# The probabilities of the cross attention: normalised on POOL, in one product with the broadcast reciprocal

## The chip, the cores and the metric

The kernel runs on one core of a Trainium2 chip. The metric is the time of one execution on the device, in microseconds (us). The core has five engines that matter here: TensorE (PE; its weight loads are listed as PEld), VectorE (DVE), ScalarE (ACT), GpSimd (POOL), and SyncE (SP), which issues most of the DMAs. Each engine works through its own queue in order, and the queues are tied by semaphores.

## What is computed

One decoder layer on x of 8 x 112 x 512 with a context of 8 x 375 x 512, all float32:

```python
x = x + attn(layernorm(x))                 # 16 heads of 32, rotary, causal
x = x + xattn(layernorm(x), ctx)           # below
x = x + ffn(layernorm(x))                  # ternary weights, silu gate

# xattn: 16 heads of 128 in 8 groups; self part and cross part, then one projection
q, k, v = fp8-quantised projections of ln(x);   q, k layer-normed
core = softmax(q k^T / sqrt(128)) v                      # over 112 tokens
kx, vx = projections of ctx;  qx, kx layer-normed
xout = softmax(qx kx^T / sqrt(128)) vx                   # over 375 context rows
out  = quantise(concat(core, xout)) @ wproj^T * scales
```

The change is in the softmax of the cross part: 8 batches x 16 heads = 128 matrices of 112 x 375.

## The kernel before, in words

The program has three stretches. Until about 210 us it does the first attention. Then come the self parts and the cross parts of the second attention, each in two halves of the heads ("halves" S0, S1, X0, X1; X0 from about 470 to 785 us, X1 to about 1095 us), each half over 8 batches. The feed-forward part follows, and its first steps overlap the end of X1.

In the stretch with the halves a planner in Python emits everything. It walks through ticks. In each tick it goes through the list `order` (L1333) and emits, for each entry (kind, lag, function), the step of the item that is due by that lag. Since each engine has one queue and works in order, the order of emission is the order of work. Per tick there is one item of projection (`p_...`), one head of attention (`t_...`) and sometimes a background unit (`b_...`) that prepares weights. In a cross half a batch has 8 projection items (q0, q1, k0, k1, k2, v0, v1, v2) and 8 heads, so it takes 8 ticks.

The steps of one cross head, with their lags behind the tick of the head:

- `t_s0` (lag 0): PE makes the scores (L1000), DVE their negated maximum (L1002), ACT the exponential with its sum (L1003) into a buffer `p` of the ring `pr`, which has two slots.
- `t_s1` (lag 1): DVE takes the reciprocal of the sum (L1017) and scales `p` with it (L1023) into a buffer `hl` of the ring `hlr`, two slots. Then the slot of `pr` and that of the small numbers (`small2`, 5 slots) are released.
- `t_s2` (lag 3): PE transposes `hl` in three pieces (L1035); DVE copies them (L1052) in X0, ACT (L1050) in X1.
- `t_s3` (lag 4): product with v (L1070), once for two heads. `t_s4` (lag 5): every fourth head, quantisation of the result (`quant`, L665: DVE L672 to L675, POOL L676 and one or two of L678). `t_s6` (lag 8): projection (L1122), once a batch.

The steps of the projection: PE L891 or L901, DVE statistics (L415, L418), `p_rstd` with ACT L426, L427 and POOL L432, L433 (for q and k, not for v), then ACT L830 and, transposed (L841), L847.

The background units of kind "t" prepare ternary weights of the feed-forward part: PE L356, ACT L359, DVE L369 to L371, POOL L372 and L373, all of `b_2` from L369 on, then DVE L380. In X0 and the first batch of X1 four ticks of eight have such a unit. The units of kind "w" split weights into two bf16 parts; for some of them POOL does the subtraction (L340, in `b_1`).

What POOL gets in one tick is thus, in the order of `order`: L432 and L433 (`p_rstd`), L676 and L678 (`t_s4`), L372 and L373 (`b_2`), anything from `t_s1`, and L340 (`b_1`). PE gets L1035, L1000, L841, L1122, L1070, L891 or L901, and L356.

PSUM has eight banks of 512 columns, taken from one pool in the order in which they come free; a bank of the scores is released by the exponential L1003.

Of the kernel before, what the change touches and what calls it, by code (L numbers as in the profile page):

```python
# [9 lines left out]
ALU = mybir.AluOpType  # L10
# [4 lines left out]
T = 112  # L15
# [105 lines left out]
def decoder_layer(nc, x, ctx_t, w_a, w_s, w_x, w_p, w_g, w_d, vec, bias, cst, cst2, scr, xs, out):  # L121
    ctx = ExitStack()
    with ctx:
        def sem(name):
            return ctx.enter_context(nc.semaphore(name))
# [4 lines left out]
        pe, act, dve, pool = (Queue(sem(f"s_{n}")) for n in ("pe", "act", "dve", "pool"))  # L130
# [842 lines left out]
        def p_head(p, hh):  # L973
            v = p[0:T, 120 * hh:120 * hh + 119]
            return bass.AP(v.tensor, v.offset, [list(v.ap[0]), [17, 7], [1, 16]])
# [35 lines left out]
        def t_s1(it):  # L1011
            S = it["bt"]["k"] == "S"
            sm, p = it["sm"], it["p"]
            n = 2 if S else 1
            w = T if S else SC
            ri = sm[0:T, 4:4 + n]
            tr = dve(lambda e: e.reciprocal(ri, sm[0:T, 2:2 + n]), it["te"])  # L1017
            hi_i, hl, hf = hlr.take()
            for j in range(n):
                dst, src = hl[0:T, w * j:w * j + w], p[0:T, w * j:w * j + w]  # L1020
                if S:
                    dst, src = dst.rearrange("p (a n) -> p a n", a=7), p_head(p, j)
                tl = dve(lambda e, j=j, dst=dst, src=src: e.tensor_scalar(  # L1023
                    dst, src, ri[:, j:j + 1], None, ALU.mult), tr, hf)
            pr.release(it["pi"], tl)
            small2.release(it["mi"], tl)
            it.update(hl=hl, hli=hi_i, tl=tl)
# [302 lines left out]
        for u in bg[LEAD + 7][16:]:  # L1330
            u["free"] = lambda: a_end
        spill_ring = Ring([f32(a, 256) for a in (aFR, aFR + 256, aCX, aCX + 256)])
        order = [("p", 1, p_stats), ("p", 1, p_vhi), ("a", 3, t_s2), ("a", 0, t_s0), ("p", 1, p_rstd), ("a", 5, t_s4),  # L1333
                 ("p", 3, p_t), ("b", 6, b_4), ("b", 3, b_2), ("a", 1, t_s1), ("p", 1, p_z), ("a", 8, t_s6),
                 ("a", 4, t_s3), ("p", 0, p_mm), ("b", 2, b_m), ("b", 4, b_3), ("b", 1, b_1), ("b", 0, b_0)]
        every = tuple(range(8))
# [167 lines left out]
```

How the kernel before makes its waits and increments, by code:

```python
    def emit(self, eng):  # L63
        for need, make, inc in self.items:
            last = {}
            for t in need:
                last[id(t.sem)] = t
            for t in last.values():
                eng.wait_ge(t.sem, t.value)
            ins = make(eng)
            if inc:
                ins.then_inc(self.sem, 1)
# [1331 lines left out]
        def run_dma(eng, items):  # L1404
            for waits, dst, src, s in items:
                for t in waits:
                    eng.wait_ge(t.sem, t.value)
                eng.dma_start(dst, src).then_inc(s, 16)
# [1 line left out]
        @block.sync  # L1410
        def _(eng):
            run_dma(eng, sync_items)
            eng.wait_ge(s_out, 16 * (NB - 1))
```

## Time and profile before

| | |
|---|---|
| time, median of 3 runs | 1215.86 us (1215.51 to 1218.77) |
| the profiled execution, its own time | 1215.43 us |
| its span, first to last instruction | 1213.1 us |
| PE busy | 1150.4 us (95%) |
| DVE busy | 920.6 us (76%) |
| ACT busy | 809.5 us (67%) |
| POOL busy | 608.9 us (50%) |
| mean granted TensorE clock | 0.983 of full speed |

The durations below come from the profiled execution, whose time differs from the median by 0.4 us. Its own time is 2.3 us more than its span. A busy PE is one with a matmul in flight. The granted clock is told as a share of 2.4 GHz.

### The profile page before, as it was taken

What the parts mean: (1) busy time and instruction counts of PE and PEld (TensorE: products, weight loads), DVE (VectorE), ACT (ScalarE), POOL (GpSimd) and SP (SyncE); (2) the same over time, 40 slices, a digit from 0 to 9 for tenths busy, and PEclk for the clock granted to TensorE, in tenths of its full rate; (3) what the DMA queues carried; (4) which work ended last, traced back from release to release, by engine and by line L of the source; (5) the groups of instructions that cost most, each with busy time, mean ns of one, the idle gap of its engine ahead of it and who ended that gap; (6) DMA issues with size and microseconds to landing.
All of it is one profiled execution on the core that took longest, in us unless ns stands there. A gap on an engine that the chain in (4) does not pass through costs nothing.

```text
span 1213.1 us, 19327 instructions
## 1 busy us (share of the span) xinstructions
PE 1150.4 (95%) x6330; PEld 764.5 (63%) x6330; DVE 920.6 (76%) x2801; ACT 809.5 (67%) x2316; POOL 608.9 (50%) x769
## 2 busy tenths in 40 slices
PE   4889988789999999999999999999999999999998
PEld 2657756556666666666666766667666666554564
DVE  4668977999878876898999989987887546586252
ACT  4667658777878876677667766678776678566140
POOL 1546984653544555454566656444544112257172
PEclk9989989899999999999999999999999999999999
DMA  8220010211211221213232232226111000000000
GB/s 273 88 60 25 26 34 17 86 51 56 70 36 36 60 84 48 79 43 108 92 113 77 69 103 74 78 70 208 61 44 52 1 2 1 1 1 1 36 1 27
DMA packets 30788, 72.41 MB, mean 60 GB/s; under 512 B 3184, under 2 KB 12528, under 8 KB 30688
## 3 DMA queue, kind: packets, MB, share of 16 engines
q1 hardware_dynamic: 30416, 70.82, 18.5%
q8 instruction: 50, 0.82, 0.3%
q14 instruction: 50, 0.41, 0.1%
q10 hardware_dynamic: 272, 0.36, 0.1%
HBM read 62.78 MB, written 8.39 MB: 59 GB/s over the span
## 4 chain that ended last, share of the span: by engine, by line
PE 59%; DVE 19%; ACT 12%; POOL 7%; issue 1%; DMA 1%; ACTq 0%; POOLq 0%; SPq 0%
PE ps L901 14%; PE ps L1194 8%; PE ps L1122 8%; PE ps L891 7%; PE ps L1070 5%; PE ps L1000 4%; PE ps L1263 4%; ACT big L830 4%; PE ps L1035 3%; PE ps L841 3%; DVE big L415 2%; DVE big L1023 2%; POOL big L699 2%; DVE big L243 1%; POOL big L698 1%
## 5 line engine op out<-in xcount | busy, mean ns | idle before, releaser
L901 PE MATMUL ps<-big 128*125 128x512 bf16 x1152 | 264.6, 379 | 1.4 <-ACT big L830 1.3
L830 ACT ACTIVATE big<-ps,big 112x128 f32<-112x128 f32 (+1 forms) x512 | 192.8, 456 | 71.6 <-POOL big L433 68.9
L901 PEld LDWEIGHTS ps<-big 128*125 128x125 bf16 x1152 | 155.1, 136 | 81.9 <-ACT big L830 1.9
L432 POOL TENSOR_TENSOR big<-big 112x4 f32<-112x4 f32 (+1 forms) x128 | 37.5, 293 | 327.2 <-ACT big L427 327.1
L891 PE MATMUL ps<-big 128*112 128x512 bf16 x768 | 187.9, 388 | 5.4 <-ACT big L994 2.1
L891 PEld LDWEIGHTS ps<-big 128*112 128x112 bf16 x768 | 100.1, 133 | 70.7 <-issue 7.7
L1003 ACT ACTIVATE big<-ps,big 112x375 f32<-112x375 f32 x128 | 74.6, 583 | 91.0 <-DVE big L1002 90.3
L415 DVE BATCH_NORM_STATS2 big<-ps 112x6 f32<-112x128 f32 (+1 forms) x512 | 113.2, 283 | 20.3 <-PE ps L901 17.3
L1070 PE MATMUL ps<-big 125*128 125x224 f32 (+1 forms) x512 | 121.1, 359 | 5.3 <-DVE big L1052 4.3
L1023 DVE TENSOR_SCALAR big<-big 112x112 f32<-112x112 f32 (+1 forms) x256 | 120.0, 490 | 6.8
L1000 PE MATMUL ps<-big 128*112 128x375 f32 x256 | 102.1, 480 | 0.9 <-ACT big L830 0.9
L1070 PEld LDWEIGHTS ps<-big 125*128 125x128 f32 (+1 forms) x512 | 91.4, 191 | 17.2 <-DVE big L1052 6.1
L1122 PE MATMUL ps<-big 128*128 128x512 bf16 x448 | 101.2, 379 | 1.0 <-ACT big L994 0.9
L1194 PE MATMUL ps<-big 128*128 128x512 bf16 (+1 forms) x512 | 99.1, 352 | 0.0
L676 POOL TENSOR_TENSOR big<-big 128x448 f32<-128x448 bf16 x64 | 62.9, 982 | 70.1 <-DVE big L1017 67.3
L1035 PEld LDWEIGHTS ps<-big 112*125 112x125 f32 (+1 forms) x512 | 78.5, 175 | 30.2 <-DVE big L1023 4.2
L847 ACT ACTIVATE big<-ps,big 128x448 f32<-128x448 f32 (+1 forms) x128 | 94.4, 737 | 0.0
L1002 DVE TENSOR_REDUCE big<-ps 112x1 f32<-112x375 f32 x128 | 68.2, 533 | 34.4 <-PE ps L1000 34.1
L1035 PE MATMUL ps<-big 112*125 112x112 f32 (+1 forms) x512 | 85.2, 268 | 1.7 <-DVE big L1023 1.6
L678 POOL TENSOR_TENSOR big<-big 128x448 bf16<-128x448 f32 (+6 forms) x112 | 82.7, 756 | 5.0
L510 PE MATMUL ps<-big 128*112 128x512 bf16 x288 | 74.9, 409 | 7.5 <-DVE big L243 4.2
L1194 PEld LDWEIGHTS ps<-big 128*128 128x128 bf16 x512 | 50.0, 98 | 45.9 <-issue 0.9
(122 smaller groups left out, 2323.6 us busy)
## 6 DMA issues: line engine op xcount, KB each, us to landing
big<-in_ctx_t SPq DMA_DIRECT2D x32, 375.0 KB, 3.4
big<-in_w_s SPq DMA_DIRECT2D x16, 512.0 KB, 4.4
big<-in_w_p SPq DMA_DIRECT2D x16, 512.0 KB, 4.3
big<-in_w_x SPq DMA_DIRECT2D x16, 512.0 KB, 3.7
big<-in_w_g SPq DMA_DIRECT2D x16, 512.0 KB, 4.0
scr<-big SPq DMA_DIRECT2D x36, 128.0 KB, 1.7
big<-scr SPq DMA_DIRECT2D x9, 512.0 KB, 8.6
big<-in_w_d SPq DMA_DIRECT2D x8, 512.0 KB, 4.8
```

The source lines that it names most:

```text
L415: t = dve(lambda e, j=j: e.bn_stats(st[:, j, :], src[0:rows, width * j:width * j + width]), toks, free)
L678: t5 = pool(lambda e, dst=dst, lo=lo, hi=hi: e.tensor_tensor(dst, t3[:, :, lo:hi], m3[:, :, lo:hi], ALU.subtract), t4, free_dst)
L830: t = act(lambda e, j=j: e.activation(z[0:rows, 128 * j:128 * j + 128], bk[0:rows, 128 * j:128 * j + 128], ACT.Identity, bias=rr[0:rows, 4 ...
L847: tf = act(lambda e: e.activation(dst, b3, ACT.Identity, bias=bb, scale=w), t, free_dst, t_qsb)
L891: t = pe(lambda e, k=k, s=s, n=n: e.matmul(bk[0:T, :], xq[:, k, :], w[:, s, k, col:col + 512], start=n == 0, stop=n == 7), xq_tok[(v, b)], ...
L901: t = pe(lambda e, k=k, s=s, u=u, n=n: e.matmul(bk[0:CK, :], cT[:, s, k, CK * c:CK * c + CK], w[:, u, k, col:col + 512], start=n == 0, sto ...
L1000: t = pe(lambda e: e.matmul(bk[0:T, 0:SC], q[:, h, :], kk[:, g, :], start=True, stop=True), bt["ready"], free)
L1023: tl = dve(lambda e, j=j, dst=dst, src=src: e.tensor_scalar(dst, src, ri[:, j:j + 1], None, ALU.mult), tr, hf)
L1035: t = pe(lambda e, j=j: e.transpose(bb[0:rows, T * j:T * j + T], hl[0:T, rows * j:rows * j + rows], identf[0:T, 0:T]), it["tl"], free, sig ...
L1070: t = pe(lambda e, c=c: e.matmul(bk[:, o:o + 224], v[0:rows, c, 128 * g:128 * g + 128], pT[0:rows, 224 * c:224 * c + 224], start=c == 0, s ...
L1122: t = pe(lambda e, h=h, s=s, n=n: e.matmul(bk, cat[:, h, :], hf["wp"][:, s, h, :], start=n == 0, stop=n == 15), tile["toks"], free, ready[ ...
L1194: t = pe(lambda e, k=k, s=s, n=n, bk=bk, which=which: e.matmul(bk[:, 0:w], wg[:, k, 2048 * which + 128 * m:2048 * which + 128 * m + 128], ...
```

## The change

In `t_s1` the scaling of the cross heads leaves DVE. Instead of DVE's tensor_scalar, with the reciprocal as the scalar of each partition, POOL does one tensor_tensor product of `p` with the reciprocal broadcast over 375 columns. The reciprocal itself stays on DVE. The new product waits for the reciprocal, for the exponential (`it["te"]`) and for its slot of `hlr`; the slots of `pr` and `small2` are now released by POOL. The self heads (S) keep their two scalings on DVE. Nothing else is touched: 128 instructions of DVE become 128 of POOL, at the place that `t_s1` has in the order.

```diff
@@ -1016,12 +1016,14 @@
             ri = sm[0:T, 4:4 + n]
             tr = dve(lambda e: e.reciprocal(ri, sm[0:T, 2:2 + n]), it["te"])
             hi_i, hl, hf = hlr.take()
-            for j in range(n):
-                dst, src = hl[0:T, w * j:w * j + w], p[0:T, w * j:w * j + w]
-                if S:
-                    dst, src = dst.rearrange("p (a n) -> p a n", a=7), p_head(p, j)
-                tl = dve(lambda e, j=j, dst=dst, src=src: e.tensor_scalar(
-                    dst, src, ri[:, j:j + 1], None, ALU.mult), tr, hf)
+            if S:
+                for j in range(2):
+                    tl = dve(lambda e, j=j: e.tensor_scalar(
+                        hl[0:T, w * j:w * j + w].rearrange("p (a n) -> p a n", a=7), p_head(p, j), ri[:, j:j + 1],
+                        None, ALU.mult), tr, hf)
+            else:
+                tl = pool(lambda e: e.tensor_tensor(hl[0:T, 0:w], p[0:T, 0:w], ri.broadcast_to([T, w]), ALU.mult),
+                          tr, it["te"], hf)
             pr.release(it["pi"], tl)
             small2.release(it["mi"], tl)
             it.update(hl=hl, hli=hi_i, tl=tl)
```

## Rows read from the trace of the kernel before

**Rows 1.** The page: busy us, share of the span and instructions of each engine.

```profile
PE 1150.4 (95%) x6330; PEld 764.5 (63%) x6330; DVE 920.6 (76%) x2801; ACT 809.5 (67%) x2316; POOL 608.9 (50%) x769
```

**Rows 2.** Stretches: length; busy of PE, PEld, DVE, ACT, POOL; granted clock; DMA share, GB/s.

```profile
628.00:667.00 39.00, 38.65 (x200) 26.38 (x198) 36.11 (x107) 26.97 (x69) 22.27 (x26) 1.00 0.29 88
892.00:929.00 37.00, 37.00 (x191) 25.50 (x190) 28.65 (x93) 26.87 (x71) 17.69 (x24) 1.00 0.14 42
965.00:1002.00 37.00, 37.00 (x192) 25.68 (x191) 20.85 (x80) 25.64 (x70) 6.69 (x16) 1.00 0.00 1
```

**Rows 3.** Waits: waiting line, releaser: us in total, times, longest us.

```profile
POOL big L432 <- ACT big L427: 327.1, 121, 17.8
...
PE ps L1070 <- DVE big L1052: 4.3, 4, 1.5
...
PE ps L1035 <- DVE big L1023: 1.6, 4, 0.5
```

**Rows 4.** Groups by form, DVE: busy us, mean ns of one | idle before.

```profile
L1023 DVE TENSOR_SCALAR big<-big 112x375 f32<-112x375 f32 x128 | 83.8, 655 | 4.6
```

**Rows 5.** Groups by form, POOL.

```profile
L540 POOL TENSOR_TENSOR big<-big 112x256 f32<-112x256 f32 x32 | 27.9, 893 | 0.0
...
L1239 POOL TENSOR_TENSOR big<-big 128x384 f32<-128x384 f32 x15 | 12.4, 827 | 8.7 <-DVE big L1230 8.7
```

**Rows 6.** Instructions in time, DVE: start, us taken, what [idle before <-releaser].

```profile
602.99 0.42 DVE L1023 TENSOR_SCALAR big<-big 112x375 f32<-112x375 f32 x1
...
619.76 1.33 DVE L1023 TENSOR_SCALAR big<-big 112x375 f32<-112x375 f32 x1
```

**Rows 7.** Instructions in time, POOL.

```profile
497.47 1.16 POOL L373 TENSOR_TENSOR big<-big 128x512 bf16<-128x512 bf16 x1
...
604.88 1.15 POOL L373 TENSOR_TENSOR big<-big 128x512 bf16<-128x512 bf16 x1
...
607.63 0.87 POOL L433 TENSOR_SCALAR big<-big 125x4 f32<-125x4 f32 x1
...
612.26 0.68 POOL L432 TENSOR_TENSOR big<-big 125x4 f32<-125x4 f32 x1 [1.40 <-ACT big L427]
...
616.28 1.53 POOL L372 TENSOR_TENSOR big<-big 128x512 bf16<-128x512 bf16 x1
617.89 1.48 POOL L373 TENSOR_TENSOR big<-big 128x512 bf16<-128x512 bf16 x1
619.73 1.15 POOL L372 TENSOR_TENSOR big<-big 128x512 bf16<-128x512 bf16 x1 [0.36 <-DVE big L1017]
...
859.46 1.19 POOL L678 TENSOR_TENSOR big<-big 128x64 bf16<-128x64 f32 x2
```

**Rows 8.** Instructions in time, PE.

```profile
84.52 0.77 PE L631 MATMUL ps<-big 112*112 112x32 f32 x3 [3.77 <-DVE big L619]
...
497.50 0.48 PE L1035 MATMUL ps<-big 112*125 112x112 f32 x3
...
547.45 2.28 PE L1070 MATMUL ps<-big 125*128 125x224 f32 x6 [1.10 <-DVE big L1052]
...
616.75 0.48 PE L1035 MATMUL ps<-big 112*125 112x112 f32 x3
...
628.83 0.80 PE L1000 MATMUL ps<-big 128*112 128x375 f32 x2
...
859.03 0.48 PE L1035 MATMUL ps<-big 112*125 112x112 f32 x3
```

**Rows 9.** Instructions in time, ACT.

```profile
606.16 0.59 ACT L1003 ACTIVATE big<-ps,big 112x375 f32<-112x375 f32 x1
...
631.41 0.57 ACT L1003 ACTIVATE big<-ps,big 112x375 f32<-112x375 f32 x1 [1.84 <-DVE big L1002]
```

**Rows 10.** Stretches, columns as in rows 2.

```profile
547.00:552.00 5.00, 4.55 (x14) 3.16 (x15) 3.51 (x10) 4.11 (x9) 2.30 (x2) 0.66 0.88 266
84.50:90.00 5.50, 5.48 (x20) 4.01 (x21) 4.82 (x8) 2.98 (x12) 4.68 (x4) 0.50 0.06 25
```

## The prediction

> **What bounds the kernel now.** I read the page first, then the stages, the waits, and last the order of instructions of one batch on each engine. The page says that TensorE (PE) is busy 95% of 1213.1 us at a granted clock of nearly full speed [rows 1]. The stages show where the change falls. While a batch of the first cross half runs, PE is busy 38.65 of 39 us, VectorE (DVE) 36.11 and POOL 22.27; in the second half PE is at 37.00 of 37, and DVE falls from 28.65 to 20.85 once the background work has ended, with POOL at 6.69 [rows 2]. So PE ends every batch; DVE stands close behind it in the first half and far behind in the second. The waits agree: PE waited 1.6 us in all for L1023, the line that is changed, and 4.3 for the copy L1052 [rows 3]. Two things follow. Time taken from DVE can be worth only what PE waits for DVE, and anything that makes PE wait is lost in full.
>
> **Part 1, what leaves DVE.** 128 scalings of 112x375 leave it: mean 655 ns, 83.8 us of busy time in all [rows 4]. They lie beside PE's work. Their price on the path is the 1.6 us in which PE waited for them [rows 3]; I credit 1.6. The self parts keep their two scalings per item and their order, and the reciprocal L1017 stays on DVE, so they cost nothing new; what hides them is unchanged.
>
> **Part 2, the new product on POOL.** No row shows a 112x375 product with a broadcast second operand. From below: the 128x384 product L1239 took a mean of 827 ns, so 375 columns are 0.81 us. From above: the rotary product L540, 112x256 with a broadcast sine, took a mean of 893 ns, which by columns is 1.31 for 375 [rows 5]. Both means hold collisions with DVE. I take 0.90, nearer to L1239, whose operands are plain rows as here; the range keeps 0.81 to 1.31. 128 x 0.90 = 115 us more on POOL. That is 8 x 0.9 = 7.2 us in a batch, so POOL goes from 22.3 to 29.5 of 39 us [rows 2]: by busy time there is room. Busy time isn't what decides, though; the queue is.
>
> **Part 3, where it stands in the queues.** POOL works in the order of emission. In each tick that order is: the two small steps L432 and L433 of the layer norm; the three steps L676, L678, L678 of a quantisation (every fourth head); the ternary subtract and add L372, L373, where a background unit is due; then t_s1's product of the head of the tick before; then L340. On DVE the scaling stood behind the ternary steps of DVE and was done early. On POOL it stands behind L373. Behind the new wait (for L1017 and L1003) only L340 and the next tick's L432 are queued, and the reciprocal is ready long before POOL gets there: the scaling behind it began at 602.99, and POOL's L373 of that tick ended at 604.88 + 1.15 = 606.03 [rows 6, 7]. So the added wait itself costs nothing. What costs is the place. Three parties wait for the product: PE's transposes L1035 two ticks on, the exponential L1003 two heads on (pr has two slots, freed by the product), and the ring hlr.
>
> Take the fourth batch, which stands for the pattern. Its fourth head's transposes start on PE at 616.75 [rows 8], and PE didn't wait for the scaling there. POOL, in the queue ahead of the new product, has seven instructions from 612.26 on, and the last, L373, ends at 617.89 + 1.48 = 619.37 [rows 7]. With 0.08 to the next start (as from 616.28 + 1.53 = 617.81 to 617.89) and 0.90 the product ends at 620.35: PE waits 3.6 us. This isn't cured by a faster product; POOL is 2.6 us late before it even begins. The same subtraction (end of L373, plus 0.98, less the start of L1035) for the nine batches in which a ternary unit meets a quantisation, at the fourth head (the third in the first batch), gives 2.1, 3.1, 3.9, 3.6, 3.7, 3.3, 3.7, 2.6 and 2.6; the first is 497.47 + 1.16 + 0.98 - 497.50 [rows 7, 8]. Sum 28.6. Once PE has waited, the heads that follow are covered: the next one would be late by 2.3 us by the same working, less than the 3.6 already given. After the ninth batch the ternary units are thinner. One place is left, the last of ten: 859.46 + 1.19 + 0.98 - 859.03 = 2.6 [rows 7, 8]. From 965 us on POOL has time to spare (6.69 busy of 37 us [rows 2]) and the product is hidden; if that cover went, 0.9 per head would be the price. Stalls: 31.2 us.
>
> **Part 4, what a stall does to PE's clock.** At 547.45 PE starts after 1.10 us of waiting [rows 8]. In the 5 us from 547 on the granted clock has a mean of 0.66 [rows 10], so for part of them the lower of its two levels, 1.2 in place of 2.4 GHz; 0.34 x 5 = 1.7 us of work lost. After PE's 3.77 us stall before 84.52 [rows 8] the clock was 0.50 for all of the next 5.5 us [rows 10]. So I expect stalls of 3 us to bring the low clock. I charge 1.7 us to nine of the ten stalls, the first of 2.1 us left out: 15.3.
>
> **Sum.** 31.2 + 15.3 - 1.6 = 44.9. The profiled execution took 1215.43 (span 1213.1 and 2.3 around it), the median of the three runs was 1215.86, so the profile stands for them within 0.4. 1215.4 + 44.9 = 1260.3.
>
> **What the sum leaves out**, in both directions. Down: with the scaling gone DVE is earlier. L1003 now starts at 631.41 where its scores began on PE at 628.83, 2.6 us before [rows 8, 9]; the scores need 0.80 of that and the maximum on DVE about 0.6; so up to 1.1 us per batch may come back, 11 in all. Up: the second head of a batch frees pr at 606.03 + 0.98 = 607.0, for an exponential that started at 606.16 [rows 7, 9], 0.9 late, and the third head likewise; that delays L427 and so POOL's L432 behind it, by up to 1.7 per batch, 15 in all. I let the two cancel.
>
> The Trainium skill (SBUF — State Buffer, Who interferes with whom) has a rule on such pairs: a VectorE tensor_scalar in a 2-port mode and any GpSimd instruction exclude each other, and whoever is first holds the pair to its end. The trace agrees: L1023 took 0.42 at 602.99 and 1.33 at 619.76, where POOL's L372 had begun at 619.73 and held it for 1.15 [rows 6, 7]. By that rule the move takes one party of such collisions away, for POOL too: L433 took 0.87 at 607.63, while a scaling ran on DVE [rows 7]. At up to 0.6 for one of them in each of ten batches the sum would be 1254 in place of 1260.
>
> **The rivals.** (a) *Late product, with the low clock*: the forecast, 1260. For it: the order in the queue is fixed by the code, and POOL is late before the product starts. Against it: one execution's spacing. (b) *Late product, clock mostly held*: 1215.4 + 29.6 - about 5 of the give-back = 1240. For it: the trace shows few stalls, and no rule for the fall. Against it: both stalls of rows 8 were followed by it. (c) *POOL becomes the bound of the first half*: exponential, L427, L432 to L373, product, next exponential is a ring from tick to tick. With 1.7 us more per batch, the product at 1.31 and two low stretches for one stall: 44.9 + 15 + 4 + 15 = 79, 1294. Against it: three ticks of each batch have no such chain, and PE lets POOL catch up. (d) *Absorbed*: PE's transposes find their product in time because DVE, relieved, runs the whole ring about 3 us earlier; -1.6 and a stall or two left over, 1216. For it: DVE loses 5 us of work per batch (8 x 0.655). Against it: POOL waits for L427 on ACT, not for DVE [rows 3]. The Trainium skill (Perfetto Trace Analysis, Optimizing Scalar/DVE Operations) warns that moving work between these two engines might not help since they share a port; its outcome, gain and loss alike, would be this one. (e) *Faster*: all that PE waits for DVE's L1023 and L1052 goes, 1.6 + 4.3 = 5.9 us [rows 3], and no transposes are late; 1209.5. It decides only if POOL reaches the product before PE reaches L1035 in the quantisation tick, 3.6 us sooner than now. (f) The change doing nothing is excluded: all 128 heads take the new branch.
>
> **How the numbers follow.** (a) 0.60, (b) 0.20, (c) 0.10, (d) 0.06, (e) 0.04. A measurement of this kernel tells 0.3%, 3.6 us, from no change. (a), (b), (c) are slower: 0.90; (d) same: 0.06; (e) faster: 0.04. Predicted is (a), 1260. The range goes from 1230, just below (b) with all 11 us given back and no low clock (1215.4 + 29.6 - 11 = 1234), to 1285, in the lower part of (c). Outside are (d), (e) and most of (c), under 2 in 10.
>
> **What would show it.** In the trace after: the waits list PE L1035 for POOL with some 30 us in ten or so long waits of 2.5 to 4.5 us, all between 495 and 860 us; the product at 0.81 to 0.95 us when free; the chain of waits through POOL's L372, L373, L676 and L678 once per batch; the granted clock at 0.5 for 3 us after each; batches of the first half 42 to 43 us apart in place of 38, those after 965 us still 36.7. Wrong would be: L1035 never waiting for POOL; waits at PE for banks (L841, L1000 for ACT) in its place, which would mean that the ring of pr bites first; or batches after 965 us longer, which would mean that POOL's place costs even where nothing stands ahead of it.

## The result, and the profile after

The changed kernel took 1247.02 us (median of four runs, 1244.78 to 1248.37) against 1215.94 for the kernel before: ratio 1.0252, 95% interval 1.0237 to 1.0267. That is 31.1 us slower. The profiled execution took 1246.97 us, its span is 1245.0, 31.9 more than before [rows 1]. In the changed kernel the scaling on POOL is L1025; lines behind it have moved by two, so the transposes are L1037, the copy L1054, the product with v L1072. The experiments move them again: in their rows a wait of the transposes for the product always has the form PE ps L10xx <- POOL big L10xx.

The page of the changed kernel, busy time of each engine:

```profile
span 1245.0 us, 19667 instructions
PE 1152.6 (93%) x6330; PEld 760.6 (61%) x6330; DVE 894.2 (72%) x2673; ACT 813.3 (65%) x2316; POOL 688.1 (55%) x897
```

PE was idle 1245.0 - 1152.6 = 92.4 us, before 1213.1 - 1150.4 = 62.7 [rows 1]: 29.7 of the 31.9 us are PE standing still. Who it waited for is in the waits of the changed kernel (waiting line, releaser: us in total, times, longest):

```profile
POOL big L432 <- ACT big L427: 284.2, 121, 8.2
...
ACT big L1003 <- POOL big L1025: 66.1, 55, 3.5
...
PE ps L1037 <- POOL big L1025: 30.2, 23, 2.9
```

L1037 waited 30.2 us for the new product, where L1035 had waited 1.6 for DVE [rows 3]. The exponentials, L1003, waited another 66.1, a row that doesn't exist before. Stretches of the changed kernel that answer to rows 2 (length; busy of PE, PEld, DVE, ACT, POOL; granted clock):

```profile
643.00:682.00 39.00, 35.97 (x183) 24.24 (x182) 32.49 (x91) 26.18 (x65) 26.12 (x34) 1.00 0.23 70
937.00:974.00 37.00, 36.15 (x184) 24.51 (x183) 24.86 (x82) 25.22 (x68) 21.19 (x31) 1.00 0.14 42
997.00:1034.00 37.00, 37.00 (x192) 25.61 (x191) 17.28 (x72) 25.57 (x70) 12.77 (x24) 1.00 0.00 1
```

Most of the loss is in the first cross half (PE 35.97 of 39 us where it was 38.65 [rows 2]): 22.7 us of the 30.2 us of waits. The other 7.5 are in the first part of the second half, and nothing in its last part, where the ternary units have ended: PE 37.00 of 37 with POOL's work nearly doubled. POOL isn't full in any of these stretches: 26.12 of 39 us.

The batch that answers to the one shown before, POOL in order of time (start, us taken):

```profile
621.32 0.20 POOL L432 TENSOR_TENSOR big<-big 125x4 f32<-125x4 f32 x1 [1.26 <-ACT big L427]
621.60 0.37 POOL L433 TENSOR_SCALAR big<-big 125x4 f32<-125x4 f32 x1
621.94 1.16 POOL L676 TENSOR_TENSOR big<-big 128x448 f32<-128x448 bf16 x1
623.18 1.45 POOL L678 TENSOR_TENSOR big<-big 128x128 bf16<-128x128 f32 x2
624.58 1.20 POOL L372 TENSOR_TENSOR big<-big 128x512 bf16<-128x512 bf16 x1
625.86 1.48 POOL L373 TENSOR_TENSOR big<-big 128x512 bf16<-128x512 bf16 x1
627.30 0.99 POOL L1025 TENSOR_TENSOR big<-big 112x375 f32<-112x375 f32 x1
```

and PE and ACT at the same place:

```profile
628.34 0.58 PE L1037 MATMUL ps<-big 112*125 112x112 f32 x3 [2.86 <-POOL big L1025]
```

```profile
620.15 0.57 ACT L1003 ACTIVATE big<-ps,big 112x375 f32<-112x375 f32 x1 [0.60 <-POOL big L1025]
...
628.38 0.57 ACT L1003 ACTIVATE big<-ps,big 112x375 f32<-112x375 f32 x1 [3.22 <-POOL big L1025]
```

Here is the whole ring of one tick, a circle of steps in which each waits for the one before: exponential at 620.15, L427, POOL from 621.32 to 628.29 without a pause, then the next exponential at 628.38, whose slot of `pr` the product has just freed. That is 8.2 us, and PE and ACT both stand at its end.

### The profile page after: what moved, and what is told of

Same layout as the page of the kernel before. It is cut to its first block, busy times and chain, and to the rows that moved or that the text cites. A ratio compares the mean times of both kernels' runs of the same rounds, so it can differ in the third digit from the quotient of the medians.

```text
span 1245.0 us, 19667 instructions
## 1 busy us (share of the span) xinstructions
PE 1152.6 (93%) x6330; PEld 760.6 (61%) x6330; DVE 894.2 (72%) x2673; ACT 813.3 (65%) x2316; POOL 688.1 (55%) x897
## 4 chain that ended last, share of the span: by engine, by line
PE 54%; POOL 16%; DVE 15%; ACT 11%; issue 2%; DMA 1%; ACTq 0%; POOLq 0%; SPq 0%
PE ps L901 11%; PE ps L1196 8%; PE ps L1124 8%; PE ps L891 7%; PE ps L1072 5%; PE ps L1000 4%; PE ps L1265 4%; PE ps L1037 3%; ACT big L830 3%; POOL big L373 2%; POOL big L1025 2%; PE ps L841 2%; ACT big L1003 2%; POOL big L372 2%; DVE big L415 2%
## 5 line engine op out<-in xcount | busy, mean ns | idle before, releaser
L432 POOL TENSOR_TENSOR big<-big 112x4 f32<-112x4 f32 (+1 forms) x128 | 34.6, 271 | 284.3 <-ACT big L427 284.2
L1003 ACT ACTIVATE big<-ps,big 112x375 f32<-112x375 f32 x128 | 73.8, 577 | 143.3 <-DVE big L1002 75.4
L415 DVE BATCH_NORM_STATS2 big<-ps 112x6 f32<-112x128 f32 (+1 forms) x512 | 113.2, 283 | 28.3 <-PE ps L901 22.7
L1025 POOL TENSOR_TENSOR big<-big 112x375 f32<-112x375 f32 x128 | 112.7, 883 | 36.0 <-DVE big L1017 36.0
L1072 PE MATMUL ps<-big 125*128 125x224 f32 (+1 forms) x512 | 120.1, 357 | 4.1 <-DVE big L1054 3.2
L1037 PEld LDWEIGHTS ps<-big 112*125 112x125 f32 (+1 forms) x512 | 76.7, 175 | 66.5 <-POOL big L1025 43.6
L1037 PE MATMUL ps<-big 112*125 112x112 f32 (+1 forms) x512 | 87.3, 272 | 30.5 <-POOL big L1025 30.2
L1072 PEld LDWEIGHTS ps<-big 125*128 125x128 f32 (+1 forms) x512 | 90.9, 190 | 15.3 <-DVE big L1054 4.2
L678 POOL TENSOR_TENSOR big<-big 128x448 bf16<-128x448 f32 (+6 forms) x112 | 78.3, 717 | 5.0
```

The source lines that it names most:

```text
L415: t = dve(lambda e, j=j: e.bn_stats(st[:, j, :], src[0:rows, width * j:width * j + width]), toks, free)
L1003: te = act(lambda e: e.activation(p[0:T, 0:SC], bk[0:T, 0:SC], ACT.Exp, bias=sm[0:T, 0:1], accum_out=sm[0:T, 2:3]), tm, pf)
L1025: tl = pool(lambda e: e.tensor_tensor(hl[0:T, 0:w], p[0:T, 0:w], ri.broadcast_to([T, w]), ALU.mult), tr, it["te"], hf)
L1037: t = pe(lambda e, j=j: e.transpose(bb[0:rows, T * j:T * j + T], hl[0:T, rows * j:rows * j + rows], identf[0:T, 0:T]), it["tl"], free, sig ...
L1072: t = pe(lambda e, c=c: e.matmul(bk[:, o:o + 224], v[0:rows, c, 128 * g:128 * g + 128], pT[0:rows, 224 * c:224 * c + 224], start=c == 0, s ...
```

## The experiments

The theory after this look was *place*: the loss is PE waiting for a product that stands behind other work in POOL's queue. The first rival was *load*: 113 us more work on POOL and its collisions with DVE, wherever the product stands. Later the theory was split: *fixed place* (only what stands ahead of the product in its own tick counts, as the prediction's sum had it) against *ring* (each tick's product also delays the next exponential and with it POOL's next tick). Each round of runs timed the kernel before again on the same chip, with medians of 1214.68, 1214.81 and 1215.61 us; every cost below is the difference to the one of its own round, and "came back" is what is missing from the 31.1 us.

**The product ahead of the ternary steps.** Steps for cross heads alone are called `s1_cross`, the self heads stay where they were.

```diff
-                 ("p", 3, p_t), ("b", 6, b_4), ("b", 3, b_2), ("a", 1, t_s1), ...
+                 ("p", 3, p_t), ("b", 6, b_4), ("a", 1, s1_cross), ("b", 3, b_2), ("a", 1, s1_self), ...
```

> Edit to the changed kernel: for the cross heads the step t_s1 (reciprocal on DVE, product on POOL) is emitted before the ternary steps of the tick (L372, L373 on POOL), still behind L432, L433 and the quantisation. Theory 'place' (the 31 us are PE waiting for a product that stands behind L373): in the tick that held PE longest the product now ends 2.4 us sooner, so of the 2.5 to 2.9 us of each long wait 0 to 0.5 is left; PE waits for POOL's product under 5 us in all, time 1214 to 1222. Rival 'load' (the cost is 113 us more work on POOL and its collisions with DVE, wherever it stands): the product is as long and as frequent, time stays at 1235 to 1247.

Measured: 1243.02 us, ratio 1.0236 (1.0220 to 1.0251). I was wrong: the cost is 28.3 us, some 3 less than before the move, and the two intervals overlap (1.0237 to 1.0267 for the changed kernel), so even that gain isn't clear. The waits, and the quantisation tick of the fifth batch (the one above was of the fourth):

```profile
PE ps L1037 <- POOL big L1025: 16.0, 19, 3.2
```

```profile
663.02 0.33 POOL L432 TENSOR_TENSOR big<-big 125x4 f32<-125x4 f32 x1 [2.17 <-ACT big L427]
663.43 0.22 POOL L433 TENSOR_SCALAR big<-big 125x4 f32<-125x4 f32 x1
663.62 1.47 POOL L676 TENSOR_TENSOR big<-big 128x448 f32<-128x448 bf16 x1
665.17 1.36 POOL L678 TENSOR_TENSOR big<-big 128x192 bf16<-128x192 f32 x2
666.49 1.26 POOL L1025 TENSOR_TENSOR big<-big 112x375 f32<-112x375 f32 x1
```

The product's inputs are old by then (its exponential was one tick before), yet POOL stands idle for 2.17 us at L432, which waits for ACT's newest work, and the product stands behind it and behind the quantisation. L373 was only part of the queue that matters; PE's waits for the product fell from 30.2 to 16.0, and others took part of their place (L1072 for the copy 4.9, L841 for ACT 2.0 us). These rows don't account for all of the time: why 14 us less of this wait gave only some 3 us stays open.

**The product first in its tick.**

```diff
-                 ("a", 3, t_s2), ("a", 0, t_s0), ("p", 1, p_rstd), ... ("a", 1, t_s1), ...
+                 ("a", 3, t_s2), ("a", 1, s1_cross), ("a", 0, t_s0), ("p", 1, p_rstd), ... ("a", 1, s1_self), ...
```

> Edit to the changed kernel: for the cross heads t_s1 is emitted directly behind t_s2, so POOL's product stands first in its tick, ahead of L432, L433, the quantisation and the ternary steps. Theory 'place': PE never waits for the product, exponentials hardly do; time 1210 to 1217, at or a little under the kernel before since DVE is relieved. What could spoil it: L432 now stands behind a product that waits for its slot of hlr (PE's transposes) and so ACT's L830 may come 0.8 us later; then 1216 to 1222 with waits for POOL's L433. Rival 'load': 1235 to 1247.

Measured: 1216.72 us, ratio 1.0013 (1.0002 to 1.0023). From its waits and from POOL's order:

```profile
PE ps L1037 <- POOL big L1025: 0.9, 2, 0.5
```

```profile
609.06 0.81 POOL L1025 TENSOR_TENSOR big<-big 112x375 f32<-112x375 f32 x1 [0.67 <-DVE big L1017]
610.63 0.33 POOL L432 TENSOR_TENSOR big<-big 125x4 f32<-125x4 f32 x1 [0.75 <-ACT big L427]
```

Now the product lies in time in which POOL waited for L427 anyway. The cost is 2.0 us by the medians, 0.13% by the ratio, so 29 of the 31 us are gone, with the same instructions on the same engines. *Load* falls for this kernel as the cause of the 31 us.

**The same order with the scaling on DVE**, the control.

> Edit to the kernel before: the same move of t_s1 for the cross heads as in the run e2_early (directly behind t_s2), with the scaling still on DVE. It shows what the order alone is worth. Theory 'place': the scaling was early enough already, PE waited 1.6 us for it in all, and now DVE's maximum stands behind it by 0.4 to 0.6 us; time 1212 to 1222, so that a difference between e2_early and this run is the engine's, not the order's. Rival ('order': moving t_s1 early is by itself worth 10 us or more): under 1206 here.

Measured: 1231.97 us, ratio 1.0142 (1.0126 to 1.0157): 17 us slower than the kernel before, outside what I expected. Two rows name waits that are new or longer:

```profile
L1023 DVE TENSOR_SCALAR big<-big 112x375 f32<-112x375 f32 x128 | 84.1, 657 | 24.4 <-PE ps L1035 20.3
```

```profile
PE ps L901 <- ACT big L1003: 3.7, 7, 0.9
```

In this place the scaling needs the slot of hlr that PE's transposes of the same tick release, and DVE stood 20.3 us behind that. But all fifteen of these waits lie behind 850 us, none in the first half, where the batches had grown too, from 38 to 39 us. There the new wait is PE's for a PSUM bank that an exponential frees (six of the seven lie there): DVE's maximum now stands behind the scaling, so the exponential comes later. PE never waited for the scaling itself. How the 17 us divide between the two isn't shown, and the last batch alone, beside the first feed-forward steps, took 8 us more. So the early order isn't good by itself: it cost 17 us with the scaling on DVE and 2 with it on POOL. What e2_early gained is not an effect of the order alone.

**Extra load that nobody waits for.** DVE scales as before; POOL does one more product from constants. In a second run (e9_shadow_first) it is emitted behind `t_s0` and ahead of `p_rstd`, so that it is the first of its tick on POOL, and waits for the exponential in place of the reciprocal.

```diff
+            if not S:
+                shadow[0] = pool(lambda e: e.tensor_tensor(f32(aFR + 512, SC)[0:T], big[0:T, aCF:aCF + SC],
+                                 cf[0:T, C_UNIT:C_UNIT + 1].broadcast_to([T, SC]), ALU.mult), tr, shadow[0])
             pr.release(it["pi"], tl)
```

> Edit to the kernel before: DVE still scales; beside that POOL does one more product of 112x375 with a broadcast column for each cross head, from constants into a spare area, at the place in POOL's queue at which the change puts its product. Nobody waits for it. It changes nothing of the result. Theory 'place': POOL is as loaded as in the changed kernel (some 690 us) but PE waits for no product; time 1214 to 1222, the few us being L432 and L340 behind it and DVE's two-input steps blocked by it. Rival 'load': DVE keeps its 84 us and POOL has 113 more, so all collisions are there and more: 1240 or above.

> Edit to the kernel before: the extra POOL product of the run e4_shadow (nobody waits for it, DVE still scales), now emitted first in its tick, ahead of L432. The earlier run had it behind the ternary steps and took 23 us. Theory 'place and DVE': POOL's load is the same, but the product no longer stands in one row with L372 and L373 against DVE's scaling; it can start before L427 is done, in POOL's idle time. Time 1216 to 1226. Rival 'load': the collisions with DVE count wherever the product stands; 1232 to 1242.

Measured: 1237.88 us at the change's place (ratio 1.0194, 1.0177 to 1.0211) and 1233.87 when it stands first in its tick (1.0151, 1.0134 to 1.0168). Both were above what *place* expected; the second is within what *load* expected, the first just under it. The groups of DVE and the waits of PE, first of the late one, then of the early one:

```profile
L1024 DVE TENSOR_SCALAR big<-big 112x375 f32<-112x375 f32 x128 | 114.5, 894 | 4.5
...
PE ps L1038 <- DVE big L1024: 12.4, 8, 2.3
```

```profile
L1024 DVE TENSOR_SCALAR big<-big 112x375 f32<-112x375 f32 x128 | 105.2, 822 | 4.5
...
PE ps L1036 <- DVE big L1024: 11.7, 8, 2.0
```

DVE's scaling grew from a mean of 655 ns [rows 4] to 894 and 822 with nothing changed but POOL's extra product, and PE waited for it eight times, once a batch, at the fifth head, where it had waited 0.3 to 0.6 us in four batches before. So *load* is real where DVE keeps the scaling: it then hits the engine that PE next waits for. Here it cost 18 to 23 us, of which these waits are about half; the rest has no single row. In the changed kernel this scaling has left DVE, and other lines have grown in its place: L380 went from a mean of 454 to 886 ns, L349 from 296 to 496, L370 from 807 to 983.

```profile
L370 DVE SCALAR_TENSOR_TENSOR big<-big 128x512 bf16<-128x512 bf16 x48 | 47.2, 983 | 1.6
...
L380 DVE SCALAR_TENSOR_TENSOR big<-big 128x256 uint32<-128x256 uint32 x48 | 42.5, 886 | 0.9 <-POOL big L373 0.5
...
L349 DVE TENSOR_SCALAR big<-big 128x256 uint32<-128x256 uint32 x48 | 23.8, 496 | 8.6 <-ACT big L329 7.6
```

That is the changed kernel. DVE gave away 83.8 us [rows 4] and is only 920.6 - 894.2 = 26.4 us less busy [rows 1]; these three lines alone took back 48 x (0.432 + 0.200 + 0.176) = 38.8. One of them, L380 at 627.62, took 2.07 us, while POOL was in the product and then in L372. In the changed kernel PE doesn't wait for them.

**Ring or fixed place: a product of 8 columns.**

```diff
-                tl = pool(lambda e: e.tensor_tensor(hl[0:T, 0:w], p[0:T, 0:w], ri.broadcast_to([T, w]), ALU.mult),
+                n_short[0] += 1
+                m = SC if n_short[0] < 3 else 8
+                tl = pool(lambda e: e.tensor_tensor(hl[0:T, 0:m], p[0:T, 0:m], ri.broadcast_to([T, m]), ALU.mult),
```

> Edit to the changed kernel: from the third cross head on POOL's product takes 8 of the 375 columns only; its place, its waits and those who wait for it stay. The rest of the normalisation is left out. Theory 'ring' (the product lengthens a ring: exponential L1003, L427, POOL's L432 to L373, product, next exponential but one, in which each tick adds its own product): five products of 0.8 us fall away before the long wait of a batch, so of its 2.5 to 2.9 us at most 0.7 is left; PE waits for the product under 8 us in all, time 1216 to 1226. Rival 'fixed place' (as the prediction worked it out: end of L373 plus one product, less the start of L1037): only one product of 0.7 us falls away per wait, 2 us are left of each, time 1237 to 1242.

Measured: 1222.22 us, ratio 1.0059 (1.0044 to 1.0074). PE's waits for the product, with the transposes at L1041:

```profile
PE ps L1041 <- POOL big L1029: 12.8, 11, 2.0
```

A fixed place would have given back ten times 0.6 to 0.7 us, 7 in all; 24 came back. The products of the ticks before count too: *ring*. This run alone doesn't prove it, since it also takes load away: POOL is 71.8 us less busy than in the changed kernel (616.3 for 688.1) and DVE 38.7 (855.5 for 894.2). In detail *ring* was off as well, since 12.8 us of waits were left where I expected under 8.

**A third slot for the exponentials.** It cuts the ring's link from the product to the exponential two heads on.

```diff
+            if not S and not prx:
+                prx.append(Ring([*pr.slots, f32(aFR + 512, 376)]))
+                prx[0].free = [*pr.free, []]
-            pi, p, pf = pr.take()
+            pi, p, pf = (pr if S else prx[0]).take()
```

> Edit to the changed kernel: the cross heads have three slots for their exponentials in place of two, so L1003 waits for a product one head older. Theory 'ring': ACT waited 66 us for POOL's product in the changed kernel; with that link cut, L427 and POOL's L432 come sooner in the quantisation tick, by up to the 1.3 us that POOL idled before L432, so each long wait shrinks from 2.9 to about 1.6; time 1230 to 1238. Rival 'fixed place': the product stands behind L373 as before, and PE waits as long; 1243 to 1248.

Measured: 1229.03 us, ratio 1.0119 (1.0104 to 1.0134). PE's waits for the product:

```profile
PE ps L1042 <- POOL big L1030: 17.2, 18, 2.1
```

Some 17 us came back from the slot alone, a little more than *ring* expected, with the product still in its late place and POOL and DVE about as busy (696.7 and 887.3 us). Neither *fixed place* nor *load* can give this; it is the cleanest evidence for the ring. At the places of the eight long waits, 2.5 to 2.9 us in the changed kernel, PE waits 0.9 to 1.5 here.

**The product twice.**

```diff
+            if not S:
+                tl = pool(lambda e: e.tensor_tensor(hl[0:T, 0:w], p[0:T, 0:w], ri.broadcast_to([T, w]), ALU.mult), tl)
             pr.release(it["pi"], tl)
```

> Edit to the changed kernel: POOL does each cross product twice in a row, and everyone waits for the second. It asks what a longer stall does to the clock. Theory 'ring': each batch of the first half gains 0.9 us in each of four to five ticks, waits of 4 to 6 us, and behind stalls that long PE's clock falls to 0.5 for 3 us each time, which it did not behind those of 2.5 to 2.9 us: at least six falls between 500 and 900 us; time 1275 to 1300. Rival 'fixed place': one 0.9 more per long wait, 1255 to 1260. Rival on the clock: no fall, the clock stays at 1.0 from 590 us on.

Measured: 1315.64 us, ratio 1.0832 (1.0815 to 1.0848), 70 us more than with one product and more than *ring* had expected. The second product isn't hidden: its group took 112.3 us of POOL's time and cost 70.

```profile
PE ps L1039 <- POOL big L1028: 61.9, 36, 4.4
...
PE ps L1039 <- DVE big L415: 9.4, 9, 2.1
```

PE waited 61.9 - 30.2 = 31.7 us more for the product, and 9.4 more at L1039 for L415. The clock takes most of the rest: the mean granted clock of this execution is 0.965 over 1314.5 us, that of the changed kernel 0.986 over 1245.0, so 46.0 - 17.4 = 29 us more went to it, by estimate. Two of the long waits, then two stretches behind them:

```profile
601.00 0.58 PE L1039 MATMUL ps<-big 112*125 112x112 f32 x3 [3.84 <-POOL big L1028]
...
694.94 0.97 PE L1039 MATMUL ps<-big 112*125 112x112 f32 x3 [3.83 <-POOL big L1028]
```

```profile
601.00:606.00 5.00, 5.00 (x18) 3.26 (x19) 3.57 (x5) 2.89 (x7) 4.84 (x5) 0.66 0.76 191
...
694.00:699.00 5.00, 4.06 (x12) 2.82 (x13) 4.38 (x6) 2.33 (x5) 4.83 (x5) 0.50 0.60 172
```

**Between: behind the scores, ahead of the layer norm.**

```diff
+                 ("a", 0, t_s0), ("a", 1, s1_cross), ("p", 1, p_rstd), ...
```

> Edit to the changed kernel: for the cross heads t_s1 is emitted behind t_s0 and ahead of p_rstd. So POOL's product stands ahead of L432 as in the run e2_early, and DVE's reciprocal behind the maximum of the next head, not before it. Theory 'head of the line' (the product suffers from whatever stands ahead of it on POOL, L432's wait for ACT included): as good as e2_early or slightly better, 1211 to 1217, PE waits for the product under 2 us. Rival: the reciprocal one step later makes exponentials wait, 1218 to 1225.

Measured: 1219.21 us, ratio 1.0032 (1.0019 to 1.0044). PE's waits for the product are 0.8 us, so the head of the line is what counts on POOL. The time lies at the lower end of the rival's range and 2.4 us above e2_early, whose interval this one's touches. Whether the reciprocal one step later is the cause I haven't isolated.

**Both cures together.** The product first in its tick and three slots.

> Edit to the changed kernel: product first in its tick (as e2_early) and three slots for the exponentials (as e6_three_p). Theory 'ring': e2_early has no wait at PE for the product worth naming (0.9 us), so the third slot has nothing left to give; 1213 to 1217, the same as e2_early and as the kernel before. Rival: what is left between e2_early and a faster kernel is still ACT waiting for the slots; then 1208 to 1212, under the kernel before.

Measured: 1217.52 us, ratio 1.0009 (0.9997 to 1.0021). No difference from the kernel before. None of the versions is faster than the kernel before.

## Why the prediction was right, point by point

**What bounds.** Right: PE bounds the cross halves, and what made it wait in the changed kernel was lost in full.

**Part 1, the credit of 1.6 us.** Right: PE no longer waited for DVE at its transposes. DVE's relief brought nothing more that the rows show; most of the busy time that DVE gave away came back on other lines, but PE had waited only 1.6 us for this one in any case.

**Part 2, the price of the product.** I took 0.90 us; the group in the changed kernel has a mean of 883 ns:

```profile
L1025 POOL TENSOR_TENSOR big<-big 112x375 f32<-112x375 f32 x128 | 112.7, 883 | 36.0 <-DVE big L1017 36.0
```

It took 0.81 us when free (609.06 in e2_early), so the lower bound by columns was exact. Single products went above the upper one, 1.31: the longest took 1.51, and the one at 881.09 in the changed kernel 1.50, before a wait of 1.48 us at PE. The mean is what the sum needed.

**Part 3, the stalls.** The sum was 31.2 us in ten waits; measured were 30.2 in 23. That it came so near is in part luck. At the ten places that I named PE waited 24.7 us (eight waits of 2.5 to 2.9, one of 1.3 and one of 1.9), 6.5 less than forecast; thirteen waits that the sum didn't have, of 0.2 to 1.5 us, gave 5.6. The place was right: in each batch of the first half the longest wait is at the transposes that I named, of the fourth head (the third in the first batch). So was the time of the product. I had it end at 620.35 where the batch's first scores began at 590.76, 29.6 us into the batch; measured, it ended at 628.29 where the batch's first scores began at 598.88, 29.4. PE reached its transposes 0.6 us later in the batch than before (26.6 us into it, where it was 26.0), so this wait was 2.86 in place of 3.6. "The heads that follow are covered" held: the next product was done at 631.92 and PE came for it at 632.41.

What was wrong in this part is the reading, not the place. I called it a matter of the last instruction ahead of the product, L373. The runs show a ring: moving the product ahead of L373 gave some 3 us at most, a third slot 17, a product of 8 columns 24, and only the place ahead of L432 nearly all of it, 29. The prediction had this ring's terms in "what the sum leaves out" (up to 1.7 per batch up, up to 1.1 down) and let them cancel. In the batch shown the ring made POOL's L432 begin 0.9 us later in the batch (22.4 us behind the first scores, where it was 21.5), and the queue from there to the end of the product was 1.1 us shorter (7.0 for 8.1). The second I hadn't forecast; it hid the first, and with it that the ring was at work. I had also said that the added wait itself costs nothing; right for the product's own wait, but the wait of L432 ahead of it is what it stands behind.

**Part 4, the clock.** This is the term that failed: 15.3 us for nine falls. There was one, behind the wait of 2.87 us before 585.55. The clock had a mean of 0.66 in the 5 us behind that, and 1.00 behind the waits of 2.81 us (before 546.56) and 2.86 us (before 628.34):

```profile
547.00:552.00 5.00, 5.00 (x28) 3.51 (x27) 4.47 (x8) 3.55 (x9) 4.57 (x5) 1.00 0.62 174
585.00:590.00 5.00, 4.45 (x15) 2.93 (x16) 4.72 (x6) 2.96 (x8) 4.57 (x5) 0.66 0.38 107
628.00:633.00 5.00, 4.66 (x25) 3.34 (x26) 4.59 (x7) 3.17 (x8) 4.57 (x5) 1.00 0.41 117
```

0.34 x 5 = 1.7 us for the one fall, as priced; the count was mis-sized, nine for one. And that one isn't even an extra: the kernel before had its own fall behind 547 [rows 10], and the changed kernel has none there. So the clock's share of the 31.1 us is about nothing; in the profiled executions its mean was 0.983 before and 0.986 after. I had gone from two stalls of the trace, of 3.8 us and of 1.1 with 0.5 before it, to a rule for all. Without part 4 the sum is 31.2 - 1.6 = 29.6, measured 31.1. That agreement is better than its parts deserve, as part 3 says.

**The rivals.** What came about is (b), the late product with the clock mostly held; I gave it 0.20 and (a) 0.60. Its time, 1240, took 5 us of give-back for DVE's relief, which didn't come. (c) was the right mechanism in a milder form: the ring makes a batch 41 us long in place of 38, without POOL being full; for the rest of the batch PE hardly waits. (d) and (e) fell. The rule of the Trainium skill (Perfetto Trace Analysis, Optimizing Scalar/DVE Operations), that moving work between DVE and POOL might not help for their shared port, fits the outcome of e2_early and e10_early_three: with nearly every wait for the product removed, 84 us taken from DVE gave nothing. That the port is the reason isn't shown, since PE had waited only 1.6 us for the scaling before [rows 3]. The other rule (SBUF — State Buffer, Who interferes with whom) pointed to a gain of 6 us from fewer collisions; measured, the long durations moved to L380, L349 and L370, and the sum got nothing from them.

## What to carry to other kernels

When a step moves to another engine, ask first what stands ahead of it in that engine's queue, the waits of those instructions included: here POOL was two thirds busy in the worst stretch and the step still cost 31 us, and moving the same step to the head of the tick brought that down to 2. In the late place its own time counts too, once in every tick of the ring: a second product there cost 70 us. Look for the ring (who waits for the step, and what that one releases back into the same queue) before subtracting times of a single tick. A place in the order that suits one engine can be harmful on another: the order that cost 2 us with the step on POOL cost 17 with it on DVE.

## What the runs showed of the hardware

PE's clock held at full speed behind seven of the eight waits of 2.5 to 2.9 us in the changed kernel, and in the run with the double product it was low behind the waits of 3.83 and 3.84 us shown above. The length of the wait alone doesn't decide it, though. In e4_shadow the clock was low behind a wait of 2.26 us, in e1_mid it stayed full behind one of 3.19 (the wait, then the 5 us behind it, first e4_shadow, then e1_mid):

```profile
709.21 0.58 PE L1038 MATMUL ps<-big 112*125 112x112 f32 x3 [2.26 <-DVE big L1024]
...
709.00:714.00 5.00, 4.66 (x14) 2.11 (x16) 4.96 (x8) 2.33 (x5) 4.98 (x5) 0.66 0.46 117
```

```profile
886.91 0.58 PE L1037 MATMUL ps<-big 112*125 112x112 f32 x3 [3.19 <-POOL big L1025]
...
887.00:892.00 5.00, 5.00 (x27) 3.46 (x28) 2.94 (x14) 4.26 (x15) 1.20 (x3) 1.00 0.01 2
```

A stall can thus cost more than its length, as it did in the run with the double product; what decides it these runs don't tell.

A POOL product of 112x375 float32 with a broadcast second operand takes 0.81 us at best and in the median (e2_early), as by columns from the 128x384 product without broadcast (a mean of 827 ns [rows 5]). Moving 128 instructions of 0.66 us from DVE to POOL lowered DVE's busy time by only a third of their sum (26.4 of 83.8 us), since other instructions of DVE took longer; the extra POOL product of e4_shadow, with nothing moved, lengthened DVE's scaling from 655 to 894 ns.
